# Taking the up half out of PSUM on ScalarE in the first four feed-forward steps

## The reference

```python
x = x + tanh(g_xattn) * xattn(layernorm(x), ctx, Wq, bq, Wk, bk)
x = x + tanh(g_ffn) * ffn(layernorm(x), w_gating, w_linear)

def xattn(logits, feats, Wq, bq, Wk, bk):       # feats: (4, 256, 128)
    q, k = feats @ Wq.T + bq, feats @ Wk.T + bk
    return logits @ softmax(q @ k.T).T

def ffn(x, w_gating, w_linear):                 # 256 -> 2 x 1024 -> 256
    gate = gelu(qdot(x, w_gating[0]))           # qdot: both sides as fp8 e4m3, result bf16
    act = gate * qdot(x, w_gating[1])
    return qdot(act, w_linear)
```

## Time and profile before

| | us |
|---|---|
| median of three runs | 52.33 |
| the profiled execution | 52.47 |
| its span, first to last instruction | 50.6 |
| TensorE busy | 42.7 (84%) |
| VectorE busy | 37.7 (75%) |
| ScalarE busy | 27.1 (54%) |
| GpSimd busy | 19.8 (39%) |

### The profile page before, as it was taken

How to read it: one execution, slowest core, us unless ns; L and a number is a source line. 1 busy time by engine, 2 the same in 40 slices (tenths; PEclk the granted TensorE clock), 3 DMA queues, 4 the chain that set the end, 5 groups by cost and what they waited for, 6 DMA issues and landing times.

```text
span 50.6 us, 859 instructions
## 1 busy us (share of the span) xinstructions
PE 42.7 (84%) x245; PEld 28.9 (57%) x245; DVE 37.7 (75%) x123; ACT 27.1 (54%) x61; POOL 19.8 (39%) x40
## 2 busy tenths in 40 slices
PE   0999999999496999974959999999999999996300
PEld 0327788877166888842414556656555869882000
DVE  2101399994897989999999699298777899789920
ACT  4512408929866991045628965984444955554000
POOL 3100186993045960576058049800000399005000
PEclk9999999999999999999999999999999999999996
DMA  0587999999999950000000000000000005420083
GB/s 0 122 271 238 342 323 289 392 237 123 106 105 104 105 47 6 0 0 0 0 0 0 13 0 0 0 0 0 0 0 0 6 23 191 136 78 0 0 298 117
DMA packets 3460, 4.64 MB, mean 92 GB/s; under 512 B 384, under 2 KB 2048, under 8 KB 3456
## 3 DMA queue, kind: packets, MB, share of 16 engines
q1 hardware_dynamic: 2592, 3.80, 22.5%
q0 software_dynamic: 864, 0.79, 16.7%
HBM read 5.90 MB, written 1.05 MB: 137 GB/s over the span
## 4 chain that ended last, share of the span: by engine, by line
PE 48%; DVE 26%; ACT 8%; DMA 5%; issue 4%; POOL 2%; DVEq 1%; ACTq 0%
PE bank L682 11%; PE bank L657 9%; PE bank L663 8%; DMA par<-params_ctxT 5%; PE bank L581 5%; DVE x L447 5%; PE bank L564 5%; PE bank L570 4%; DVE ap L476 4%; PE bank L617 3%; DVE aq L485 3%; DVE st L452 3%; DVE xh L466 3%; ACT gl L354 2%; PE bank L588 2%
## 5 line engine op out<-in xcount | busy, mean ns | idle before, releaser
L476 DVE SCALAR_TENSOR_TENSOR ap<-bank,gl 128x512 f16<-128x512 f32 (+1 forms) x20 | 11.6, 582 | 3.6 <-PE bank L663 2.7
L354 ACT ACTIVATE gl<-bank 128x512 bf16<-128x512 f32 (+1 forms) x20 | 10.0, 508 | 6.0 <-PE bank L657 6.0
L663 PE MATMUL bank<-xq,wg 128*128 128x512 fp8e4 (+1 forms) x40 | 10.2, 337 | 0.7 <-DVE ap L476 0.6
L657 PE MATMUL bank<-xq,wg 128*128 128x512 fp8e4 (+1 forms) x40 | 10.2, 337 | 0.7 <-ACT xq L345 0.7
L682 PE MATMUL bank<-wl,aq 128*128 128x256 fp8e4 x64 | 10.1, 273 | 0.7 <-DVE aq L485 0.6
L682 PEld LDWEIGHTS bank<-wl,aq 128*128 128x128 f16 x64 | 6.0, 98 | 4.1 <-DVE aq L485 1.6
L617 PE MATMUL bank<-attnT,xT_sb 128*128 128x256 f32 x32 | 7.6, 382 | 0.0
L485 DVE TENSOR_SCALAR aq<-ap 128x512 uint16<-128x512 uint16 (+1 forms) x20 | 6.9, 350 | 0.0
L617 PEld LDWEIGHTS bank<-attnT,xT_sb 128*128 128x128 f32 x32 | 5.8, 190 | 0.8 <-ACT attnT L334 0.2
L663 PEld LDWEIGHTS bank<-xq,wg 128*128 128x128 fp8e4 x40 | 3.7, 98 | 4.3 <-DVE ap L476 2.2
L279 POOL TENSOR_TENSOR yo<-ys,res 128x256 f32<-128x256 f32 x4 | 2.9, 746 | 7.3 <-ACT ys L362 7.3
(11 more groups left out here) (50 smaller groups left out, 57.8 us busy)
## 6 DMA issues: line engine op xcount, KB each, us to landing
x_sb<-x SPq DMA_DIRECT2D x4, 256.0 KB, 5.2
xT_sb<-xT SPq DMA_DIRECT2D x4, 256.0 KB, 5.7
out<-yo SPq DMA_DIRECT2D x6, 128.0 KB, 2.0
wg<-w_gating POOLq DMA_DIRECT2D x4, 128.0 KB, 7.1
par<-params_ctxT SPq DMA_DIRECT2D x1, 258.0 KB, 2.8
par<-params_ctxT SPq DMA_DIRECT2D x1, 256.0 KB, 4.5
wl<-w_linear POOLq DMA_DIRECT2D x2, 128.0 KB, 7.7
out<-yo SPq DMA_DIRECT2D x1, 256.0 KB, 2.0
```

Of the source, the lines that this page charges most:

```text
L354: nc.scalar.activation(gl[:, s % 2, toks], gate_b[s % 2][:, toks], ACT.Gelu_apprx_tanh).then_inc(gelu_ready, 1)
L476: nc.vector.scalar_tensor_tensor(ap[:, s % NAP, toks], up_b[s % 2][:, toks], ACT_SCALE, gl[:, s % 2, toks], ALU.mult, ALU.mult).then_inc(p ...
L657: mm = nc.tensor.matmul(gate_b[s % 2][:, toks], wg8[:, c, k, 0, o:o + P], xq[:, g, k, toks], start=(k == 0), stop=(k == KC - 1))
L663: mm = nc.tensor.matmul(up_b[s % 2][:, toks], wg8[:, c, k, 1, o:o + P], xq[:, g, k, toks], start=(k == 0), stop=(k == KC - 1))
```

## The change

In steps 0 to 3 a ScalarE ACTIVATE (Copy with the scale 2^-8) writes the up bank to a new SBUF tensor `up`, bfloat16, with four buffers. It stands in ScalarE's queue right behind the gelu of its step. VectorE then multiplies `up` by `gl`, two bfloat16 tensors in SBUF, and gives float16 as before. The up matmuls of steps 2 to 5 wait for that copy instead of the product. Steps 4 to 19 are as they were.

```diff
+        up = sb("up", [P, NUP, TOK], BF16)          # NUP = 4
...
+            def up_out(s):
+                act.wait_ge(up_done, s + 1)
+                nc.scalar.activation(up[:, s, :], up_b[s % 2][:, :], ACT.Copy, scale=ACT_SCALE).then_inc(up_ready, 1)
...
                 gelu(s)
+                if s < NUP:
+                    up_out(s)
...
-                nc.vector.scalar_tensor_tensor(ap[:, s % NAP, toks], up_b[s % 2][:, toks], ACT_SCALE,
-                                               gl[:, s % 2, toks], ALU.mult, ALU.mult).then_inc(prod_ready, 1)
+                if s < NUP:
+                    dve.wait_ge(up_ready, s + 1)
+                    nc.vector.tensor_tensor(ap[:, s % NAP, toks], up[:, s, toks], gl[:, s % 2, toks],
+                                            ALU.mult).then_inc(prod_ready, 1)
+                else:
+                    nc.vector.scalar_tensor_tensor(ap[:, s % NAP, toks], up_b[s % 2][:, toks], ACT_SCALE,
+                                                   gl[:, s % 2, toks], ALU.mult, ALU.mult).then_inc(prod_ready, 1)
...
-                if s >= 2:
+                if s >= NUP + 2:
                     pe.wait_ge(prod_ready, s - 1)
+                elif s >= 2:
+                    pe.wait_ge(up_ready, s - 1)
```

More of the change, by code:

```diff
@@ L53, in flamingo_block @@
     LAG = 3
+    NUP = 4
     EPS = 1e-5
@@ L184, in flamingo_block @@
         gelu_ready = sem("gelu_ready")
+        up_ready = sem("up_ready")
         prod_ready = sem("prod_ready")
```

## The result

The changed kernel is slower, by about 1.2%: 53.19 us, the median of six runs (52.83 to 54.12), against 52.36 for six runs of the kernel before. The ratio of the runs to be compared is 1.0119 with a 95% interval of 1.0067 to 1.0172. On 52.33 us that is +0.62 us (0.35 to 0.90), 52.95. The forecast was +0.40 and 52.73. The median itself, 53.19, lies 0.09 above the range of 52.30 to 53.10; the time by the ratio lies in it, though the upper end of its interval (53.23) does not. The ratios leave out disturbed executions (the two of 54.12 us among them); the profile of one experiment, e2, is of such a one, and only distances inside a stretch at the full granted clock are read from it.

A forecast was written before the change was run, and what follows sets the result against it. Two chains meet at up matmul 7, TensorE's own and one through VectorE, GpSimd and ScalarE, before TensorE turns solid. Terms 0.20 + 0.16 + 0.04 = +0.40 us on 52.33 gave 52.73 us, range 52.30 to 53.10.

The forecast's parts named there:

- What bounds the kernel: At up matmul 7, TensorE's own chain and one through VectorE, GpSimd and ScalarE meet with nothing to spare; the change lengthens the second.
- The multiply: VectorE's product in steps 0 to 3, reading two 16-bit SBUF inputs, takes 0.42 us instead of 0.69.
- rival 4: The 16-bit multiply in SBUF is no faster, 0.69 us; sum +0.67 us, time 53.00 us; chance 5%.
- Product 2: On VectorE it starts 0.47 us later behind copy 2, its shorter multiply gives some back, rounding 1 is +0.20 us.
- The first power: GpSimd's operation behind product 0 waits for that product's SBUF reads; it, norm2(2) and gelu 2 are 0.16 us later.
- that earlier rounding: On VectorE, product 1 and rounding 0 come some 0.3 us earlier, which only adds idle time before product 2: worth nothing.
- The second power: GpSimd's operation behind product 3, already lengthened to 0.81 us, makes norm2(3) 0.04 us later.
- Sum: Delay at up matmul 7: 0.20 + 0.16 + 0.04 = +0.40 us, carried whole to the end.
- Rival 2: GpSimd's powers are not touched by the new multiply; +0.20 us alone, time 52.53 us; chance 20%.
- Rival 3: GpSimd's powers stand for the whole multiply, +0.31 and +0.19 us; with 0.20, +0.70 us, time 53.03 us; chance 17%.
- Rival 1: TensorE's earlier up matmuls carry through to the end, 0.27 us faster, time 52.06 us; chance 10%.
- TensorE's guard: Up matmuls 2 to 5 wait for copies; up 4 starts 0.27 us earlier, but none is left at up 7.

The follow-up runs named there:

- e2: Kernel before with copy and 16-bit multiply in step 2 only: first finish 0.25 us later in the trace, ratio to before 1.0047.
- e6: Changed kernel, but up matmuls 2 to 5 wait for the product again: first finish 23.94 us after the first gate matmul, as in the changed kernel.
- f1: Changed kernel with VectorE's rounding 1 and moments of batch 3 moved ahead of product 2: first finish 0.50 us earlier than the changed kernel, ratio to before 1.0079.
- e3: Kernel before plus the four copies, which products wait for but do not read, still multiplying from PSUM: first finish 0.51 us later, ratio 1.0145.
- f9: f7 with rounding 0 ahead of batch 2's moments, product 3 and rounding 2 ahead of batch 3's moments: first finish 23.04 us, ratio to before 0.9902.
- e5: Kernel before with copies in steps 0 and 1 only, kept as float32: first finish 23.88 us after the first gate matmul (before 23.31), no ratio.
- f8: f9 plus the copy and 16-bit multiply in step 1 alone: first finish 22.87 us after the first gate matmul, ratio to before 0.991.
- f7: Kernel before without copies, VectorE, ScalarE and TensorE orders rearranged around batches 2 and 3: first finish 0.49 us earlier, ratio 0.995.
- f11: Kernel before, with GpSimd's last addition waiting for VectorE's last rounding: first finish 22.84 us, last store issue 0.08 us earlier, ratio 0.9965.

## Why the prediction was right, and where its sizes were off

- *What bounds the kernel.* Right: two chains meet at up 7. e6 shows that TensorE's could take 0.52 us of delay at up 4 without moving the end, f1 that freeing the other one gives 0.50 back, and e3 that TensorE's own sets the end (+0.51) once it is the later.
- *The multiply.* 0.42 was forecast and measured; rival 4 falls.
- *Product 2.* Forecast 0.47 late and 0.27 given back, +0.20. Measured 0.52 late and 0.27 given back, +0.25 (e2). The missing 0.05 lies between the copy's end and the product's start: 0.13 us (29.31 to 29.44), where I had carried over the 0.08 behind a gelu.
- *The first power.* Forecast +0.16, measured +0.21. The idea was right, that it works for 0.15 us and then waits for the product's end; the product began only 0.07 ahead of it, not 0.11. Left out altogether: nmr, 0.09 longer. It now comes 0.21 later and rounding 0 comes 0.16 earlier (26.88, less the 0.17), so the two meet: rounding 0 begins 0.05 ahead of nmr. f9, without a copy, has the same pairing at batch 3, with nmr at 0.28; where no rounding stands beside it (e2, e3) it takes 0.20. I had written of that earlier rounding that it is "worth nothing by itself". It is the largest single miss, and that sentence the step that failed: a term put at nothing that measured 0.09.
- *The second power.* Forecast +0.04, measured +0.10. Product 3 began 0.07 ahead of the power and not 0.11, which is 0.04 later in the chain, and from its start to the power's end it took 0.98 and not 0.96.
- *Sum.* 0.25 + 0.30 + 0.10 = 0.65 (0.63 to 0.64 in the trace) against 0.40. Rival 2 (GpSimd isn't touched) falls. Rival 3 would have had 0.31 for the first power, where 0.21 was measured; that nmr's 0.09 makes its number up to 0.30 is luck, and so is that its sum, +0.70, is nearer to the measured time than mine. Its rule, that GpSimd stands for the whole multiply, is right up to the 0.15 us at the start. The Trainium skill (SBUF — State Buffer, Who interferes with whom) says that a VectorE instruction with two inputs in SBUF contends with a GpSimd one that reads SBUF, and that one with a single input there, outside the modes that use both ports, does not. e3 and e5 agree: an input in PSUM frees GpSimd (0.69), two in SBUF hold it until the product's end, fast (0.90) or slow (1.17). The section has the later of the two blocked in full; here all but its first 0.15 us was. The rows by which I had weighed this show VectorE instructions with one tensor input, another pair than the product's.
- *Rival 1* falls by the result and by e6. Only in the order of f9 does a copy help TensorE (f8, 0.17 by the trace).
- *Rival 4's sum* was wrong by my own rule. A multiply of 0.69 in SBUF would have held the first power for 0.43 and not 0.16, so its total is 0.90 and more, 53.23 at least, outside the range. e5 shows such a multiply: the power took 0.48 more.
- *TensorE's guard.* Up 4 was to start 0.27 earlier; with gelu 2 late by 0.30 it started 0.03 later.

## What to carry to other kernels

Before work goes from a busy engine to an idle one, follow the chain of the stretch in which it lands: here a copy stood in ScalarE's queue ahead of what the next normalisation waited for, and VectorE's 1.1 us less of busy time bought nothing. An operation that gets its second input from SBUF instead of PSUM changes who may run beside it, and the small GpSimd operation beside it can be the one on the chain. Where two chains meet, a delay of the right size doesn't show by which of them it came (e3): look at what the last instruction waited for. Try the order of the queues first: moving calls gained 0.5 us in the trace where the copies lost 0.6.

## What the runs showed of the hardware

- A GpSimd operation on 128x2 elements takes 0.69 us alone, 0.90 or 1.17 when a product with two SBUF inputs began 0.07 us ahead of it; it ends 0.55 us after the product (0.42 or 0.69 long).
- A 16-bit rounding beside the same operation: begun 0.10 us ahead of it (f7), it leaves it at 0.72, again ending 0.54 after the rounding; begun 0.49 behind it, the operation takes 0.81 (before, e2, f8, f9); begun 0.54 behind it, 0.69 (e3). That the last two differ by what the operation does at its end is argued, not shown.
- In the other direction the last rounding takes 0.70 beside GpSimd's addition and 0.23 when the addition waits (f11).
- Left open: why the first float32 matmuls gain their full pace at different times, by which S varies by up to 1.0 us between profiles. Not tried: giving the powers to another engine.
